# Self-attention of a decoder layer: the values of two steps in one round, one pair of scores ahead of it

## The chip, the core and the metric

The kernel runs on one core of a Trainium2 chip. The metric is the device time of one execution in microseconds (us). The engines of the core are TensorE (PE, with its weight loads shown apart as PEld), VectorE (DVE), ScalarE (ACT), GpSimd (POOL) and SyncE (SP, which here issues transfers).

## The reference, cut to what matters

One decoder layer with layer norms after each part: self-attention with rotary embedding and a linear bias by distance, cross-attention, and a mixture of experts. The change touches the self-attention alone: 4 sequences of 1024 tokens, 16 heads of 16 columns.

```python
B, N, C = x.shape                                    # 4, 1024, 256
q = q * cos + _rotate_half(q) * sin
k = k * cos + _rotate_half(k) * sin
attn = jnp.einsum('bhqd,bhkd->bhqk', q, k) * SCALE
diff = pos[None, :] - pos[:, None]
diff = jnp.where(diff > 0, 0.0, diff)
alibi = diff[None, :, :] * slopes[:, None, None] * MAX_BIAS
attn = attn + alibi[None]
w = jax.nn.softmax(attn, axis=-1)
out = jnp.einsum('bhqk,bhkd->bhqd', w, v)
```

## The kernel before, in words

The stages follow one another: projections, self-attention (`stage_attention`), its output projection, cross-attention, router, experts, combination. Self-attention works on 16 groups, each of four heads of one sequence (`NG`, `HG`), in one window per group. A window has 16 steps (`STEPS`): two halves of 512 queries, and in each half 8 blocks of 128 keys.

In a step, four score tiles (128 keys by 512 queries, one per head, tiles 0 to 3) are computed, exponentiated and multiplied with the values:

- `score_pair` (L741 the product, L755 the bias) writes two tiles. Two heads lie in the two halves of PE's rows, so a pair runs side by side. Steps 0 to 3 and 12 to 15 cross the diagonal and add 6 or 12 small bias products to each tile, 12 or 24 a pair; the other eight steps add none. The tiles go round three banks (`s_ps`, `BANKS`), and `score_main` waits on `exp_done` for the tile three before.
- ACT takes the exponential of each tile (L630) into a set of four buffers, `w_exp`; there are three sets (`SETS`), and the first exponential of a step waits on `pv_done` for the values that last read its set.
- `values` (L782) multiplies the four exponentials of a step with the values into one bank, `a_ps`, summed over a half of the window. The first column beyond the head's 16 is one, so it gathers the softmax's sums.

Softmax subtracts a row's maximum, which has to be known before. So each window also makes the maxima of the next group: 32 units (`max_pair`, L712 the product, L720 the bias), each writing two banks of a ring of two slots, which DVE reduces (`maxima`, L646). Through the same ring pass the transposed tops (`transpose_top`, L770; `copy_top`, L663), sent by `move_top` (L523) into a row of the query stack, and the transposed accumulators (`transpose_acc`, L790; `normalise`, L669 and L673), which ACT has first copied out of `a_ps` (`copy_acc`, L619). The order in which these take the ring's places is written out in `ring_order`, and PE and DVE follow it.

PE's order is written by hand in `window`. Before, in step st: tiles 0 and 1, then the values of step st − 2, then a transpose if one is due, then tiles 2 and 3, then two units of maxima.

Of the kernel before, what the change touches and what calls it, by code (L numbers as in the profile page):

```python
# [408 lines left out]
STEPS = 2 * KT  # L409
TILES = 4 * STEPS  # L410
UNITS = 2 * STEPS
SETS = 3
BANKS = 3


# [8 lines left out]
TOP0_AT = 19  # L424


def ring_order(first, with_max):


    order = []  # L430
    for st in range(STEPS):
        if st == 1:
            order.append(("top", 1))
        if st == 2 and not first:
            order.append(("acc", 1))
        if st == 9 and with_max:
            order.append(("top", 0))
        if st == 10:
            order.append(("acc", 0))
        order += [("max", 2 * st + i) for i in range(2) if with_max]  # L440
    return order


# [18 lines left out]
PLACES = ring_places()  # L462


def stage_attention(nc, io, keep):
# [10 lines left out]
    with Scope(nc, "att") as s:  # L476
# [3 lines left out]
        vg = [s.sb(f"v_group{i}", [P, KT, HG * VW + 32 - VW + 1], F32) for i in range(3)]  # L480
        w_exp = [[s.sb(f"w_exp{i}{h}", [P, CH], F32) for h in range(HG)] for i in range(SETS)]
        ident, past, slope_eye = keep["ident"], keep["past_bf"], keep["slope_eye"]
# [82 lines left out]
        def _(pool):  # L565
# [23 lines left out]
            def window(g, with_max, has_last):  # L589
# [5 lines left out]
                if with_max:  # L595
                    if has_last:

                        pool.wait_ge(pv_done, STEPS * (g.n - 1) + SETS)
                    take_v(g.plus(1))
# [4 lines left out]
        @block.scalar  # L604
        def _(act):
            act.sem_inc(exp_done, BANKS)
            act.sem_inc(acc_done, 1)

            for i in (1, 2):
                for side in range(2):  # L610
                    rows = slice(64 * side + ROW_BIAS, 64 * side + ROW_LOW)
                    for j in range(2):
                        ins = nc.scalar.activation(qs[i][rows, j, :], keep["q_rows"][rows, :], ACT.Copy)
                ins.then_inc(act_prep, 1)

            def copy_acc(g, c):

                act.wait_ge(pv_done, STEPS * g.n + KT * (c + 1) + SETS)
                nc.scalar.activation(acc_sb[c][:, :], a_ps[:, :], ACT.Copy).then_inc(acc_done, 1)  # L619

            def window(g, with_max, has_last):
                for st in range(STEPS):
                    c, kt = divmod(st, KT)
                    for h in range(HG):
                        act.wait_ge(score_done, TILES * g.n + 4 * st + h + 1)
                        if h == 0:

                            act.wait_ge(pv_done, STEPS * g.n + st + 1)
                        v = TILES * g.n + 4 * st + h
                        nc.scalar.activation(w_exp[(STEPS * g.n + st) % SETS][h][:, :], s_ps[v % BANKS][:, :], ACT.Exp).then_inc(exp_done, 1)  # L630
                        if st == 1 and h == 1 and has_last:
                            copy_acc(g.plus(-1), 1)
                        if st == 9 and h == 1:
                            copy_acc(g, 0)

            windows(window)
            copy_acc(Group.of(NG - 1), 1)

        @block.vector
        def _(dve):  # L640
            dve.sem_inc(ring_free, RING_SLOTS)
            def maxima(u, place):
                dve.wait_ge(ring_full, place.at + 1)
                half, j, q, kk = max_unit(u)
                out = row_max[half][:, :, :].rearrange("p (h q) k -> p h q k", q=4)[:, 2 * j:2 * j + 2, q, kk]
                nc.vector.tensor_reduce(out, ring[place.slot][:, :, :], AX.X, ALU.max).then_inc(ring_free, 1)  # L646

            def top_parts(g, half, place):


                dve.wait_ge(ring_free, place.at + 1 + RING_SLOTS)
                nc.vector.tensor_reduce(top[:, :], row_max[half][:, :, :], AX.X, ALU.max).then_inc(top_step, 1)
                dve.wait_ge(top_step, 4 * g.n + 2 * half + 1)
                nc.vector.tensor_scalar(neg_top[:, 0, :], top[:, :], -1.0, None, ALU.mult).then_inc(top_step, 1)
                dve.wait_ge(top_step, 4 * g.n + 2 * half + 2)
                nc.vector.scalar_tensor_tensor(neg_top[:, 1, :], top[:, :], -1.0, neg_top[:, 0, :].bitcast(F32),
                                               ALU.mult, ALU.subtract).then_inc(top_ready, 1)
# [26 lines left out]

            def window(g, with_max, has_last):
                for st in range(STEPS):
                    if st == 1:
                        copy_top(g, 1, PLACES[g.n, "top", 1])
                    if st == 2 and has_last:
                        normalise(g.plus(-1), 1, PLACES[g.n, "acc", 1])  # L690
                    if st == 9 and with_max:
                        copy_top(g.plus(1), 0, PLACES[g.n, "top", 0])
                    if st == 10:
                        normalise(g, 0, PLACES[g.n, "acc", 0])
                    for i in range(2):
                        if with_max:
                            maxima(2 * st + i, PLACES[g.n, "max", 2 * st + i])
                    if with_max and st % 8 == 7:
                        top_parts(g.plus(1), st // 8, PLACES[g.n, "max", 2 * st + 1])

            windows(window)
            last = Group.of(NG - 1)
# [3 lines left out]
        def _(pe):  # L706
            pe.sem_inc(pv_done, SETS)

# [92 lines left out]
            def window(g, with_max, has_last):  # L801
                if with_max:
                    n = g.plus(1)
                    pe.wait_ge(eye_ready, g.n + 2)
                    pe.wait_ge(stack_in[n.buf], 16 * STACK_DMAS * (n.lap + 1))
                for st in range(STEPS):
                    c, kt = divmod(st, KT)
                    if kt == 0:
                        pe.wait_ge(top_in[c], 32 * g.n + 32)
                    score_pair(g, st, 0)  # L810
                    if st > 1:
                        values(g, st - 2)
                    elif has_last:
                        values(g.plus(-1), STEPS + st - 2)
                    if st == 1:
                        transpose_top(g, 1, PLACES[g.n, "top", 1])
                    if st == 2 and has_last:
                        transpose_acc(g.plus(-1), 1, PLACES[g.n, "acc", 1])
                    if st == 9 and with_max:
                        transpose_top(n, 0, PLACES[g.n, "top", 0])  # L820
                    if st == 10:
                        transpose_acc(g, 0, PLACES[g.n, "acc", 0])
                    score_pair(g, st, 2)
                    if with_max:
                        for i in range(2):
                            max_pair(n, 2 * st + i, PLACES[g.n, "max", 2 * st + i])

            windows(window)
            last = Group.of(NG - 1)
# [1656 lines left out]
```

## Time and profile before

| | us |
|---|---|
| median of 3 runs | 2145.97 |
| lowest, highest | 2145.86, 2155.84 |
| the profiled execution, its time | 2138.17 |
| the profiled execution, its span | 2136.4 |

The span is the time from the first to the last instruction of the profiled execution; some 1.8 us of its time lie around it. On the page, PE is busy for 1712.4 us of the span, DVE for 1380.1, ACT for 981.0. Busy time of PE is made of modelled ends of pipelined matmuls, so the starts of its instructions, one after another, tell more than their lengths. A row of the timeline merges like instructions that follow each other: its first number is the start of the first, its second the time to the end of the last.

### The profile page before, as it was taken

The numbers are of one execution on the slowest core, as the hardware profiler recorded it, in microseconds if no ns is written. First come the engines' busy times: TensorE is split into PE (matmuls) and PEld (weight loads), VectorE is DVE, ScalarE is ACT, GpSimd is POOL, SyncE is SP. The second block draws the span as 40 slices with busy tenths as digits, with TensorE's granted clock in tenths as the row PEclk, the third lists the DMA queues.
The fourth block names the chain that finished last, engine by engine and source line by source line (L and its number), as shares of the span: only waits on it lengthen the run. The fifth ranks groups of instructions, "written<-read, shape, count | busy, mean of one in ns | idle before, by whom it ended". The sixth has DMA issues, their size and how long they took to land. (4 is left out here: it accounts for less than half of the span.)

```text
span 2136.4 us, 39383 instructions
## 1 busy us (share of the span) xinstructions
PE 1712.4 (80%) x15124; PEld 1170.3 (55%) x15124; DVE 1380.1 (65%) x2248; ACT 981.0 (46%) x1582; POOL 418.0 (20%) x320
## 2 busy tenths in 40 slices
PE   5747999999999999984656888848874999999900
PEld 5633444444444444433545767726653888888900
DVE  5548888888888888823756787732234566556356
ACT  2312777777777777771212555523332333333100
POOL 4323000000000000001103433301442221111075
PEclk9965999999999999996877999969986999999955
DMA  6687455544445555004533112032222222222055
GB/s 195 148 172 218 66 74 70 72 63 60 59 60 74 72 74 68 16 7 115 180 123 103 57 63 74 24 105 68 87 68 96 82 82 81 81 86 86 25 161 158
DMA packets 135604, 190.89 MB, mean 89 GB/s; under 512 B 32336, under 2 KB 99296, under 8 KB 134436
## 3 DMA queue, kind: packets, MB, share of 16 engines
q1 hardware_dynamic: 128164, 167.02, 34.2%
q0 software_dynamic: 7296, 21.86, 3.2%
q8 instruction: 102, 1.67, 0.4%
q14 instruction: 42, 0.34, 0.1%
HBM read 122.93 MB, written 69.21 MB: 90 GB/s over the span
## 5 line engine op out<-in xcount | busy, mean ns | idle before, releaser
L646 DVE TENSOR_REDUCE att_row_max<-att_ring 128x2 f32<-128x1024 f32 x512 | 602.2, 1220 | 119.3 <-PE att_ring L720 59.6
L630 ACT ACTIVATE att_w_exp<-att_s_ps 128x512 f32<-128x512 f32 x1024 | 547.7, 596 | 232.7 <-PE att_s_ps L755 156.9
L782 PE MATMUL att_a_ps<-att_w_exp,att_v_group 128*32 128x512 f32 x2048 | 273.6, 606 | 0.2 <-ACT att_w_exp L630 0.2
L741 PE MATMUL att_s_ps<-att_q_stack,att_k_stack 62*128 62x512 f32 x640 | 181.4, 480 | 0.0
L741 PEld LDWEIGHTS att_s_ps<-att_q_stack,att_k_stack 62*128 62x128 f32 x640 | 84.3, 184 | 123.9 <-ACT att_w_exp L630 112.7
L2144 ACT ACTIVATE ex_hid<-ex_h_ps,ex_b 128x512 f32<-128x512 f32 x128 | 88.0, 688 | 114.4 <-PE ex_h_ps L2236 72.8
L712 PE MATMUL att_ring<-att_k_stack,att_q_stack 60*128 60x512 f32 x640 | 131.3, 450 | 6.2 <-DVE att_att L673 3.2
L568 POOL COPY att_eyes<-keep_slope_eye 128x384 bf16<-128x384 bf16 x16 | 8.1, 506 | 654.8 <-PE att_s_ps L755 632.4
L755 PE MATMUL att_s_ps<-att_eyes,keep_past_bf 64*128 64x64 bf16 x3840 | 133.0, 193 | 0.0
L741 PE MATMUL att_s_ps<-keep_q_stack,keep_k_stack 62*128 62x512 f32 x384 | 114.1, 487 | 9.9 <-ACT att_w_exp L630 6.3
L712 PE MATMUL att_ring<-keep_k_stack,keep_q_stack 60*128 60x512 f32 x384 | 89.8, 503 | 35.2 <-POOL att_eyes L568 22.0
L1368 POOL TENSOR_TENSOR cr_e<-cr_e,cr_rec 128x1232 f32<-128x1232 f32 x32 | 72.0, 2249 | 221.5 <-DVE cr_rec L1513 221.5
L755 PEld LDWEIGHTS att_s_ps<-att_eyes,keep_past_bf 64*128 64x128 bf16 x3840 | 93.3, 95 | 29.8 <-issue 15.6
L1606 PE MATMUL cr_s_ps<-cr_k_blk,cr_q 128*128 128x308 f32 (+1 forms) x384 | 84.6, 337 | 31.0 <-DVE cr_e L1501 25.6
L2176 DVE CAST ex_h_hi<-ex_hid 128x512 fp32r<-128x512 f32 x128 | 93.6, 732 | 21.4 <-ACT ex_hid L2144 21.1
L2178 DVE TENSOR_TENSOR ex_h_lo<-ex_hid,ex_h_hi 128x512 fp32r<-128x512 f32 x128 | 103.3, 807 | 4.4
L1396 ACT ACTIVATE cr_w_t<-cr_t_ps 77x1024 f32<-77x1024 f32 x64 | 61.9, 1014 | 93.7 <-PE cr_t_ps L1631 93.6
L741 PEld LDWEIGHTS att_s_ps<-keep_q_stack,keep_k_stack 62*128 62x128 f32 x384 | 51.5, 187 | 89.9 <-ACT att_w_exp L630 80.3
L2187 DVE TENSOR_TENSOR ex_y<-ex_y_ps,ex_b 128x256 f32<-128x256 f32 x64 | 26.7, 424 | 111.0 <-PE ex_y_ps L2247 111.0
L1808 POOL DMA_INDIRECT rows_scr<-ro_x_send,ro_put_u x64 | 64.9, 1014 | 152.5 <-DVE ro_put_u L1922 135.5
L2134 ACT ACTIVATE ex_x_hi<-ex_t_ps 128x1024 fp32r<-128x1024 f32 x16 | 16.4, 1026 | 159.5 <-PE ex_t_ps L2224 159.5
L1606 PEld LDWEIGHTS cr_s_ps<-cr_k_blk,cr_q 128*128 128x128 f32 x384 | 66.6, 210 | 41.1 <-issue 22.3
(268 smaller groups left out, 3875.4 us busy)
## 6 DMA issues: line engine op xcount, KB each, us to landing
first_w_raw<-ew SPq DMA_DIRECT2D x16, 1024.0 KB, 7.9
att_k_stack<-qk_scr SPq DMA_DIRECT2D x120, 128.0 KB
keep_k_stack<-qk_scr SPq DMA_DIRECT2D x72, 128.0 KB
qk_scr<-qkv_t_hi SPq DMA_DIRECT2D x64, 128.0 KB, 2.3
qk_scr<-qkv_t_lo SPq DMA_DIRECT2D x64, 128.0 KB, 2.3
rows_scr<-att_zeros POOLq DMA_DIRECT2D x8, 1024.0 KB, 22.0
cr_q<-q_scr SPq DMA_DIRECT2D x16, 512.0 KB, 5.2
ex_rows<-rows_scr SPq DMA_DIRECT2D x16, 512.0 KB, 5.9
```

The costliest lines, as they stand in the source:

```text
L630: nc.scalar.activation(w_exp[(STEPS * g.n + st) % SETS][h][:, :], s_ps[v % BANKS][:, :], ACT.Exp).then_inc(exp_done, 1)
L646: nc.vector.tensor_reduce(out, ring[place.slot][:, :, :], AX.X, ALU.max).then_inc(ring_free, 1)
L712: return nc.tensor.matmul(ring[place.slot][:, i, :], qs[g.buf][rows, j, tok:tok + P], ks[g.buf][rows, half, j, kk * CH:(kk + 1) * CH], sta ...
L741: ins = nc.tensor.matmul(s_ps[v % BANKS][:, :], ks[g.buf][rows, c, j, kt * P:(kt + 1) * P], qs[g.buf][rows, j, c * CH:(c + 1) * CH], start ...
L755: ins = nc.tensor.matmul(s_ps[bank][:, at:at + 64], past[side, far, half, :], eyes[g.buf][side, part, h // 2, :], start=False, stop=n == last)
L782: ins = nc.tensor.matmul(a_ps[32 * h:32 * h + 32, :], vg[g.buf][:, kt, h * VW:h * VW + 32], w_exp[(STEPS * g.n + st) % SETS][h][:, :], sta ...
L1368: pool.tensor_tensor(e[m % 4][:, :, :], e[m % 4][:, :, :], rec[m % 2][:, :].unsqueeze(2).to_broadcast([P, H, L]), ALU.mult).then_inc(w_don ...
L1606: nc.tensor.matmul(s_ps[k][:, half, 0:GL], q[c][a][:, k, tok], k_blk[:, b, bass.ds(i, 1), k, cols].rearrange("p o n -> p (o n)"), start=(j ...
L1808: pool.indirect_dma_start(io["rows_scr"], bass.IndirectOffsetOnAxis(put_u[c][:, 2 * t + k:2 * t + k + 1], 0), x_send[c][:, t, :], None, bo ...
L2144: nc.scalar.activation(hid[m % 2][:, :], h_ps[m % 2][:, :], ACT.Relu, bias=b1[:, bass.ds(e, 1), m:m + 1].rearrange("p a b -> p (a b)") if ...
L2176: nc.vector.tensor_copy(h_hi[c][:, m, :], hid[m % 2][:, :]).then_inc(h_hi_done, 1)
L2178: nc.vector.tensor_tensor(h_lo[c][:, m, :], hid[m % 2][:, :], h_hi[c][:, m, :].bitcast(F32), ALU.subtract).then_inc(h_lo_done, 1)
```

## The change

The values of two steps are computed together, once in two steps, behind tiles 0 and 1 of an even step. Three units of maxima follow the even step's tiles (two) and the odd step's (one), and the fourth is held back: it comes in the next even step, between tiles 0 and 1 and the values (`maxima_ahead`, `maxima_behind`). Transposes move to even steps (tops from 1 and 9 to 2 and 10, accumulators from 2 and 10 to 4 and 12), the copies of the accumulator on ACT from behind tile 1 of steps 1 and 9 to behind tile 2 of steps 0 and 8. `SETS` goes from 3 to 4.

```diff
--- before.py
+++ after.py
@@ -409,7 +409,7 @@
 STEPS = 2 * KT
 TILES = 4 * STEPS
 UNITS = 2 * STEPS
-SETS = 3
+SETS = 4
 BANKS = 3
 
 
@@ -424,20 +424,31 @@
 TOP0_AT = 19
 
 
+def maxima_ahead(st):
+
+    return [2 * st - 1] if st % 2 == 0 and st else []
+
+
+def maxima_behind(st):
+
+    return [2 * st, 2 * st + 1] if st % 2 == 0 or st == STEPS - 1 else [2 * st]
+
+
 def ring_order(first, with_max):
 
 
     order = []
     for st in range(STEPS):
-        if st == 1:
+        order += [("max", u) for u in maxima_ahead(st) if with_max]
+        if st == 2:
             order.append(("top", 1))
-        if st == 2 and not first:
+        if st == 4 and not first:
             order.append(("acc", 1))
-        if st == 9 and with_max:
+        if st == 10 and with_max:
             order.append(("top", 0))
-        if st == 10:
+        if st == 12:
             order.append(("acc", 0))
-        order += [("max", 2 * st + i) for i in range(2) if with_max]
+        order += [("max", u) for u in maxima_behind(st) if with_max]
     return order
 
 
@@ -628,9 +639,9 @@
                             act.wait_ge(pv_done, STEPS * g.n + st + 1)
                         v = TILES * g.n + 4 * st + h
                         nc.scalar.activation(w_exp[(STEPS * g.n + st) % SETS][h][:, :], s_ps[v % BANKS][:, :], ACT.Exp).then_inc(exp_done, 1)
-                        if st == 1 and h == 1 and has_last:
+                        if st == 0 and h == 2 and has_last:
                             copy_acc(g.plus(-1), 1)
-                        if st == 9 and h == 1:
+                        if st == 8 and h == 2:
                             copy_acc(g, 0)
 
             windows(window)
@@ -684,19 +695,24 @@
 
             def window(g, with_max, has_last):
                 for st in range(STEPS):
-                    if st == 1:
+                    if with_max:
+                        for u in maxima_ahead(st):
+                            maxima(u, PLACES[g.n, "max", u])
+                            if u == UNITS // 2 - 1:
+                                top_parts(g.plus(1), 0, PLACES[g.n, "max", u])
+                    if st == 2:
                         copy_top(g, 1, PLACES[g.n, "top", 1])
-                    if st == 2 and has_last:
+                    if st == 4 and has_last:
                         normalise(g.plus(-1), 1, PLACES[g.n, "acc", 1])
-                    if st == 9 and with_max:
+                    if st == 10 and with_max:
                         copy_top(g.plus(1), 0, PLACES[g.n, "top", 0])
-                    if st == 10:
+                    if st == 12:
                         normalise(g, 0, PLACES[g.n, "acc", 0])
-                    for i in range(2):
-                        if with_max:
-                            maxima(2 * st + i, PLACES[g.n, "max", 2 * st + i])
-                    if with_max and st % 8 == 7:
-                        top_parts(g.plus(1), st // 8, PLACES[g.n, "max", 2 * st + 1])
+                    if with_max:
+                        for u in maxima_behind(st):
+                            maxima(u, PLACES[g.n, "max", u])
+                            if u == UNITS - 1:
+                                top_parts(g.plus(1), 1, PLACES[g.n, "max", u])
 
             windows(window)
             last = Group.of(NG - 1)
@@ -808,22 +824,25 @@
                     if kt == 0:
                         pe.wait_ge(top_in[c], 32 * g.n + 32)
                     score_pair(g, st, 0)
-                    if st > 1:
-                        values(g, st - 2)
-                    elif has_last:
-                        values(g.plus(-1), STEPS + st - 2)
-                    if st == 1:
+                    if with_max:
+                        for u in maxima_ahead(st):
+                            max_pair(n, u, PLACES[g.n, "max", u])
+                    if st % 2 == 0 and (st or has_last):
+                        old, at = (g, st) if st else (g.plus(-1), STEPS)
+                        values(old, at - 2)
+                        values(old, at - 1)
+                    if st == 2:
                         transpose_top(g, 1, PLACES[g.n, "top", 1])
-                    if st == 2 and has_last:
+                    if st == 4 and has_last:
                         transpose_acc(g.plus(-1), 1, PLACES[g.n, "acc", 1])
-                    if st == 9 and with_max:
+                    if st == 10 and with_max:
                         transpose_top(n, 0, PLACES[g.n, "top", 0])
-                    if st == 10:
+                    if st == 12:
                         transpose_acc(g, 0, PLACES[g.n, "acc", 0])
                     score_pair(g, st, 2)
                     if with_max:
-                        for i in range(2):
-                            max_pair(n, 2 * st + i, PLACES[g.n, "max", 2 * st + i])
+                        for u in maxima_behind(st):
+                            max_pair(n, u, PLACES[g.n, "max", u])
 
             windows(window)
             last = Group.of(NG - 1)
```

PE in steps of a group without bias products, before: from the values of one step to the values of the next (L741 scores, L712 and L720 maxima, L782 values):

```order
L782 MATMUL att_a_ps<-att_w_exp,att_v_group 32x512 x4
L741 MATMUL att_s_ps<-att_q_stack,att_k_stack 128x512 x2
L712 MATMUL att_ring<-att_k_stack,att_q_stack 128x512 x2
L720 MATMUL att_ring<-att_eyes,keep_past_bf 128x64 x4
L712 MATMUL att_ring<-att_k_stack,att_q_stack 128x512 x2
L741 MATMUL att_s_ps<-att_q_stack,att_k_stack 128x512 x2
L782 MATMUL att_a_ps<-att_w_exp,att_v_group 32x512 x4
```

The same place on PE in the changed program, from one round's values to the next round's (L757 scores, L728 and L736 maxima, L798 values):

```order
L798 MATMUL att_a_ps<-att_w_exp,att_v_group 32x512 x8
L757 MATMUL att_s_ps<-att_q_stack,att_k_stack 128x512 x2
L728 MATMUL att_ring<-att_k_stack,att_q_stack 128x512 x2
L736 MATMUL att_ring<-att_eyes,keep_past_bf 128x64 x4
L728 MATMUL att_ring<-att_k_stack,att_q_stack 128x512 x2
L757 MATMUL att_s_ps<-att_q_stack,att_k_stack 128x512 x4
L728 MATMUL att_ring<-att_k_stack,att_q_stack 128x512 x2
L736 MATMUL att_ring<-att_eyes,keep_past_bf 128x64 x8
L757 MATMUL att_s_ps<-att_q_stack,att_k_stack 128x512 x2
L728 MATMUL att_ring<-att_k_stack,att_q_stack 128x512 x2
L798 MATMUL att_a_ps<-att_w_exp,att_v_group 32x512 x8
```

The values stand there eight matmuls at a time, where before four came after every four score tiles; between two such places there are now eight score tiles and four units of maxima, the last of them right ahead of the values.

ACT at the start of self-attention, before: exponentials (L630) and the first copy of the accumulator (L619):

```order
L630 ACTIVATE att_w_exp<-att_s_ps 128x512 x38
L619 ACTIVATE att_acc_sb<-att_a_ps 128x512
L630 ACTIVATE att_w_exp<-att_s_ps 128x512 x32
```

ACT in the changed program at the same place (L641 exponentials, L630 copy):

```order
L641 ACTIVATE att_w_exp<-att_s_ps 128x512 x35
L630 ACTIVATE att_acc_sb<-att_a_ps 128x512
L641 ACTIVATE att_w_exp<-att_s_ps 128x512 x32
```

The first copy comes three exponentials earlier, behind tile 2 of step 8; between two copies there are 32 exponentials in both.

## Rows read from the trace of the kernel before

**Rows 1.** The page: the span, and the clock of TensorE in 40 slices, tenths.
```profile
span 2136.4 us, 39383 instructions
...
PEclk9965999999999999996877999969986999999955
```

**Rows 2.** Windows: stretch, length, busy PE, PEld, DVE, ACT, POOL, clock, transfers (share, GB/s).
```profile
538.12:585.78 47.66, 47.03 (x590) 22.29 (x594) 40.34 (x45) 35.41 (x67) 1.09 (x2) 1.00 0.45 67
...
919.46:967.20 47.74, 41.22 (x443) 15.25 (x443) 3.50 (x10) 34.93 (x66) 0.00 (x0) 1.00 0.02 8
```

**Rows 3.** Waits in a full window, then in the last one: sum, times, longest, us.
```profile
PEld att_s_ps L741 <- ACT att_w_exp L630: 11.3, 18, 0.8
...
PEld att_ring L712 <- DVE att_row_max L646: 1.0, 2, 0.6
...
PEld att_s_ps L741 <- ACT att_w_exp L630: 22.9, 28, 1.0
```

**Rows 4.** Timeline of PE in a step without bias: start, length, instruction.
```profile
553.55 1.06 PE L782 MATMUL att_a_ps<-att_w_exp,att_v_group 128*32 128x512 f32 x8
554.55 0.50 PE L741 MATMUL att_s_ps<-att_q_stack,att_k_stack 62*128 62x512 f32 x2
554.88 0.40 PE L712 MATMUL att_ring<-att_k_stack,att_q_stack 60*128 60x512 f32 x2
555.12 0.23 PE L720 MATMUL att_ring<-att_eyes,keep_past_bf 64*128 64x64 bf16 x4
...
555.73 0.50 PE L741 MATMUL att_s_ps<-att_q_stack,att_k_stack 62*128 62x512 f32 x1
556.16 1.06 PE L782 MATMUL att_a_ps<-att_w_exp,att_v_group 128*32 128x512 f32 x8
```

**Rows 5.** Timeline of ACT in the same step, and the durations of L630.
```profile
555.08 2.06 ACT L630 ACTIVATE att_w_exp<-att_s_ps 128x512 f32<-128x512 f32 x4 [0.49 <-PE att_s_ps L741]
...
L630 ACT ACTIVATE att_w_exp<-att_s_ps x65: 592/597/618, 538.1 to 585.8; 128x512 f32<-128x512 f32 x65
```

**Rows 6.** Timelines of PE and ACT in a step with bias, last window.
```profile
919.37 1.07 PE L782 MATMUL att_a_ps<-att_w_exp,att_v_group 128*32 128x512 f32 x8
920.37 0.49 PE L741 MATMUL att_s_ps<-keep_q_stack,keep_k_stack 62*128 62x512 f32 x2
...
921.74 0.49 PE L741 MATMUL att_s_ps<-keep_q_stack,keep_k_stack 62*128 62x512 f32 x1 [0.38 <-ACT att_w_exp L630]
...
922.35 1.07 PE L782 MATMUL att_a_ps<-att_w_exp,att_v_group 128*32 128x512 f32 x8
...
921.09 1.08 ACT L630 ACTIVATE att_w_exp<-att_s_ps 128x512 f32<-128x512 f32 x2 [0.55 <-PE att_s_ps L755]
922.44 1.08 ACT L630 ACTIVATE att_w_exp<-att_s_ps 128x512 f32<-128x512 f32 x2 [0.26 <-PE att_s_ps L755]
```

**Rows 7.** Timeline of PE in the router: values-shaped matmuls on end.
```profile
1457.39 1.92 PE L1985 MATMUL ro_l_ps<-ro_hid,ro_rw 128*32 128x512 f32 x16 [0.78 <-ACT ro_hid L1830]
```

**Rows 8.** Timeline of ACT around a copy of the accumulator.
```profile
564.50 0.59 ACT L630 ACTIVATE att_w_exp<-att_s_ps 128x512 f32<-128x512 f32 x1
565.10 0.60 ACT L619 ACTIVATE att_acc_sb<-att_a_ps 128x512 f32<-128x512 f32 x1
565.72 1.08 ACT L630 ACTIVATE att_w_exp<-att_s_ps 128x512 f32<-128x512 f32 x2
```

**Rows 9.** Timelines of DVE and SyncE: tops from copy to transfer.
```profile
518.21 0.27 DVE L663 CAST att_neg_top_t<-att_ring 32x128 fp32r<-32x128 f32 x1
...
524.88 1.24 SPq L523 DMA_DIRECT2D att_q_stack<-top_scr  x2
```

**Rows 10.** Timeline of DVE: one maximum, then two on end.
```profile
555.40 1.23 DVE L646 TENSOR_REDUCE att_row_max<-att_ring 128x2 f32<-128x1024 f32 x1 [0.24 <-PE att_ring L720]
...
521.98 2.35 DVE L646 TENSOR_REDUCE att_row_max<-att_ring 128x2 f32<-128x1024 f32 x2
```

**Rows 11.** A stretch of cross-attention, columns as in rows 2.
```profile
1180.00:1230.00 50.00, 45.41 (x350) 41.07 (x343) 39.93 (x69) 25.55 (x26) 20.92 (x11) 0.97 0.21 72
```

## The prediction

> **What bounds the kernel now.** I read the page first: of the span of 2136.4 us, the slices between about 200 and 970 us are self-attention, with the clock of TensorE (PE) at 9 or more tenths [rows 1]. Cutting that stretch into the 16 windows of the program shows its rhythm. One in the middle has PE busy for 47.0 of 47.7 us, VectorE (DVE) for 40.3 and ScalarE (ACT) for 35.4; so it looks bound by PE. The second row speaks against that. The last window has no maxima to make: DVE falls to 3.5 us and PE to 41.2 us, and the window still takes 47.74 us [rows 2]. So neither PE's amount of work nor DVE sets the time, but something that both kinds of window share.
>
> The waits say what. PE waits for the exponentials (L630) 18 times in a full window, for 11.3 us, and 28 times for 22.9 us in the last one; its weight loads wait for DVE 1.0 us [rows 3]. It is a loop through PE, ACT and the three banks of scores. Call the score tiles of a step 0 to 3. A tile may be written only when the exponential of the tile three before it is done. In a step without bias products [rows 4, 5] the values begin at 553.55; the pair 2, 3 follows at 554.55 (1.00 later); its first exponential starts at 555.08 (0.53 later) and takes 0.60; tile 1 of the next step, which needs that bank, starts at 555.73 (0.05 after it), and the next values at 556.16 (0.43 later). The sum is 1.00 + 0.53 + 0.60 + 0.05 + 0.43 = 2.61 us, which is the whole step. The maxima lie in the wait. In a step with 12 bias products per pair (last window) the same loop reads 1.00, then 0.72 to the exponential, 0.65 to tile 1 at 921.74, where PE visibly waits 0.38, and 0.61 to the values: 2.98 us [rows 6]. Per window, 8 steps have such bias products (0 to 3 and 12 to 15) and 8 have none.
>
> **The change part by part.** No instruction is added or taken away. What changes is how often values stand between scores.
>
> *Two steps' values together.* The switch is cheaper: 128 times in place of 256 does PE go from scores to values and back. One step of values is two passes of four matmuls, 1.06 us in all [rows 4]. The router has matmuls of the same shape, and there four passes on end take 1.92 us [rows 7]: the two further passes cost 0.86, where a step that stands alone takes 1.00. But the loop gets longer. Take a round without bias, with t = 0 at the pair 2, 3 of the even step, right behind the double values. Until the next double values, PE must write eight tiles: 2, 3 of the even step, 0 to 3 of the odd one, 0 and 1 of the next even one. Tile 1 at the end needs the bank of tile 2 of the odd step, so five exponentials must have run: the first starts at 0.53, and four in a row take 2.06 us, so they follow each other by (2.06 − 0.60)/3 = 0.49 [rows 5]. The fifth starts at 0.53 + 4 × 0.49 = 2.49 and ends at 3.09; tile 1 starts at 3.14. Behind it stand the held-back maxima, a pair that costs 0.24 (554.88 to 555.12) [rows 4], and 0.43 to the values as before: 3.81. The double values take 1.00 + 0.86: **5.67 us a round, where two steps now take 5.22: +0.45**. The two exponentials that run under the double values fill 1.1 of its 1.9 us; ACT idles for the rest and lacks it afterwards.
>
> In a round with bias, t = 0 at the same place: first exponential at 0.72; tile 1 of the odd step waits for it until 0.72 + 0.60 + 0.05 = 1.37. A tile waited for in this way has its pair's first exponential 0.70 later (921.74 to 922.44), at 2.07 [rows 6]; tile 3 waits for that one until 2.72, the exponential of tile 2 starts at 3.42, and the next tile 1 waits for it until 4.07. From there 0.61 to the values, and about 0.3 for the maxima pair between (0.24 to 0.33, the two distances in [rows 4]): 4.98. With 1.86 of values: **6.84, against 2 × 2.98 = 5.96: +0.88**. One loop through ACT per step has become three per round. Steps with 24 bias products lengthen both sides alike.
>
> Four rounds of each kind give 4 × (0.45 + 0.88) = 5.3 us a window.
>
> *Copies of the accumulator.* They move from behind tile 1 of the odd steps 1 and 9 to behind tile 2 of steps 0 and 8, that is, into the run of exponentials that sets the time. One holds ACT from 565.10 to 565.72, 0.6 us [rows 8]. Before, it also stood in a row of exponentials, so part of that was paid already. Between 0 and 1.2 us a window, I take 0.4.
>
> *The held-back maxima* are in the sum above (0.24 or 0.3). In the last window there are none, so it grows by 4 × (0.45 − 0.24) + 4 × (0.88 − 0.3) + 0.4 = 3.6 us.
>
> *Fourth set of exponentials.* The first exponential of a step waits for values four steps back and not three. That wait is not among those listed [rows 3], so it is worth nothing. *Transposes* of tops and accumulators move one or two steps later and still stand behind values on PE: same cost. The transfer of the tops that follows, from the copy at 518.21 to the end of the last issue at 526.12 [rows 9], takes 8 us and was due at step 16 from step 9, some 20 us; with six steps left (some 16 us) it is still early, and so is SyncE's queue behind it. GpSimd's copies wait for whole windows and have a window's slack.
>
> Sum: 15 × (5.3 + 0.4) + 3.6 = **+89 us**, all in self-attention. Against the profiled execution, 2138.2 + 89 = 2227; the median of the runs stands 7.8 us above that execution, so I forecast **2235 us**, 4.1% slower. Ends of the sum: copies free and the held-back maxima at half their price (the other half under tile 1), 15 × 4.2 + 3.2 = 66; copies in full, 15 × 6.5 + 4.4 = 102.
>
> **The rivals.**
>
> *The cheaper switch decides (faster).* Where PE never waits for an exponential, each double round saves the cold entry of one values step: 1.00 − 0.86 = 0.14, the way into it (0.43 against 0.33 from pair to pair) and out of it (a first pair of 0.33 against 0.24) [rows 4]: about 0.33 × 128 = 42 us, 2104 us. The Trainium skill, "TensorEngine Tiling (Array Packing)", section "Key Properties", says that changing the tiling mode drains TensorE; by that rule alone the time would be these 2104 us. The trace agrees that the switch costs, with the distances just read. It decides from the point where the exponentials keep up with eight tiles on end. Against it stands the last window, where 6 us less work on PE gave nothing [rows 2].
>
> *The maxima's ring becomes the bound (slower still).* Two slots hold the maxima, and the held-back pair needs the slot of the one two before it. In a round without bias the first maxima start about 0.33 after t = 0, DVE begins 0.52 later (554.88 to 555.40) and needs 2.35 for two [rows 4, 10]: the slot is free at 3.25, and the held-back pair's turn comes behind tile 1 at 3.14, whose own 0.24 covers the rest. 0.2 us more per round would be 24 us: 2259.
>
> *The clock falls (slower still).* PE would idle about as in the last window, where the clock stayed at 1.00 [rows 2]; in cross-attention, with PE busy for 45.4 of 50 us, it was 0.97 [rows 11]. Three per cent on some 850 us is 25 us at most: 2260. The skill's "TensorE: Matmul & The Clock Gate", section on psum-queue depth-cycling, names short idle times between groups of matmuls as a cause of such falls.
>
> *Nothing happens.* The loop is absorbed in the waits that PE has now, 11.3 us a window [rows 3]: 2146. That would need ACT to run further ahead than three banks let it.
>
> **How the numbers follow.** Forecast 0.74, ring 0.10, clock 0.08: slower by over 0.5%, which is about what a measurement of this kernel can tell from no change, 0.92. Nothing 0.04, faster 0.04. The range takes in the lower end of the sum on the lower base (2138 + 66 = 2204) and the two slower rivals with some room (2259 and 2260): 2204 to 2265. The upper end of the sum on the higher base, 2146 + 102 = 2248, lies inside.
>
> **What would show it.** After the change, windows of self-attention of some 53 us, PE busy for less of them, ACT at 35 us as before; a round without bias of 5.7 us, two runs of values touching, and in the gap two exponentials; waits of score tiles for L630's successor at 20 us or more a window; DVE idle longer. Wrong is the forecast if windows get shorter than 47.7 us, if the long waits are DVE's for PE or PE's for DVE, or if the clock leaves 1.00. Right in the total but wrong in its parts would be rounds with bias that grow no more than those without.

## The result, and the profile after

The changed kernel takes 2255.3 us (median of 4 runs, 2250.89 to 2260.16) against 2145.91 us: the ratio is 1.051, with a 95% interval of 1.0455 to 1.0565. The forecast was 2235 us, in a range of 2204 to 2265.

The page of the changed kernel, the lines that answer to [rows 1]:

```profile
span 2257.4 us, 39383 instructions
...
PEclk9966999999999999999686899977996999999955
```

Self-attention's slices still read 9 tenths. Each digit is the mean of a slice of 56 us, and it hides something, as the windows show. They are cut at the first exponential of each group, with the columns of [rows 2]:

```profile
477.05:531.81 54.76, 52.40 (x590) 25.22 (x594) 40.85 (x45) 34.45 (x66) 1.09 (x2) 0.97 0.41 58
...
584.98:638.12 53.14, 50.81 (x590) 24.77 (x594) 40.73 (x45) 34.45 (x66) 1.09 (x2) 1.00 0.41 60
1019.88:1075.00 55.12, 48.58 (x439) 18.65 (x443) 3.52 (x10) 34.36 (x66) 0.00 (x0) 0.91 0.02 7
```

There are two lengths of full windows. Three take 53.15 us at a clock of 1.00, 5.5 us more than before. Eleven take 54.8 us or so, and their clock is 0.97. The first takes 56.0 us (from 49.6); it starts at a low clock in both kernels, and shows the same fall as the eleven. The last window, up to the end of its values (the row above stops 0.7 us earlier), takes 55.8 us (from 47.7) at 0.91.

A round without bias in the changed kernel, the timelines of PE and then of ACT (steps 6 and 7 of the group that begins at 584.98), which answer to [rows 4, 5]:

```profile
605.43 1.92 PE L798 MATMUL att_a_ps<-att_w_exp,att_v_group 128*32 128x512 f32 x16
607.28 0.51 PE L757 MATMUL att_s_ps<-att_q_stack,att_k_stack 62*128 62x512 f32 x2
...
610.43 0.50 PE L757 MATMUL att_s_ps<-att_q_stack,att_k_stack 62*128 62x512 f32 x1
610.56 0.60 PE L728 MATMUL att_ring<-att_k_stack,att_q_stack 60*128 60x512 f32 x2
611.09 1.92 PE L798 MATMUL att_a_ps<-att_w_exp,att_v_group 128*32 128x512 f32 x16
...
604.10 2.08 ACT L641 ACTIVATE att_w_exp<-att_s_ps 128x512 f32<-128x512 f32 x4
607.82 4.03 ACT L641 ACTIVATE att_w_exp<-att_s_ps 128x512 f32<-128x512 f32 x8 [1.65 <-PE att_s_ps L757]
```

From values to values it is 611.09 − 605.43 = 5.66 us; the working gave 5.67. The values of two steps take 1.85 us to the next pair (1.86). The bracket on ACT's second row is the price: ahead of eight exponentials on end, 4.03 us, ACT has had nothing to do for 1.65 us. From the start of the last tile ahead of the values to the first exponential behind them it is 0.66 + 1.85 + 0.54 = 3.05 us (610.43 to 611.09, 605.43 to 607.28, 607.28 to 607.82), and the three banks hold three exponentials for that time, at 0.49 us each. Before, ACT waited 0.49 us in each step.

The twelve windows with a fall differ from the three at one place, around the values of step 10. The timeline of PE, first in such a window, then in one of the three:

```profile
509.88 3.04 PE L798 MATMUL att_a_ps<-att_w_exp,att_v_group 128*32 128x512 f32 x16
512.85 0.29 PE L786 MATMUL att_ring<-keep_ident,att_neg_top 128*32 128x128 f32 x1
...
564.17 1.92 PE L798 MATMUL att_a_ps<-att_w_exp,att_v_group 128*32 128x512 f32 x16
566.02 0.28 PE L786 MATMUL att_ring<-keep_ident,att_neg_top 128*32 128x128 f32 x1
```

The same 16 matmuls take 1.1 us longer. The stretch shows why (three pieces of it):

```profile
502.00:505.40 3.40, 3.40 (x35) 1.29 (x32) 3.30 (x6) 1.92 (x4) 0.00 (x0) 1.00 1.04 128
505.40:508.80 3.40, 2.92 (x19) 1.38 (x16) 2.79 (x4) 3.23 (x7) 0.00 (x0) 0.99 1.04 124
508.80:512.20 3.40, 3.40 (x19) 1.23 (x23) 2.10 (x2) 1.28 (x3) 0.00 (x0) 0.50 0.58 75
```

PE's clock is at 0.50 (1.2 GHz, not 2.4) from 508.8 to 512.2. Ahead of it lies step 9, where PE was busy for 2.92 of 3.40 us; it stood for 0.48 us in front of a score tile:

```profile
507.20 0.98 PE L757 MATMUL att_s_ps<-att_q_stack,att_k_stack 62*128 62x512 f32 x2 [0.48 <-ACT att_w_exp L641]
```

A window with this fall is 1.62 us longer, and there are 12 of them in this execution.

So the sum is: 15 full windows by 5.5 us, 82.5; 12 falls by 1.62, 19.4; the last window 8.1. That is 110 us. From the end of attention's values (967.2 before, 1075.7 after) the trace gives 108.5, and the medians 109.4.

### The profile page after: what moved, and what is told of

It is laid out like the page before. It is cut to its first block and busy times, and to the rows that moved or that the text cites. A ratio compares the mean times of both kernels' runs of the same rounds, so it can differ in the third digit from the quotient of the medians.

```text
span 2257.4 us, 39383 instructions
## 1 busy us (share of the span) xinstructions
PE 1795.6 (80%) x15124; PEld 1213.1 (54%) x15124; DVE 1386.3 (61%) x2248; ACT 965.1 (43%) x1582; POOL 416.0 (18%) x320
## 5 line engine op out<-in xcount | busy, mean ns | idle before, releaser
L641 ACT ACTIVATE att_w_exp<-att_s_ps 128x512 f32<-128x512 f32 x1024 | 539.0, 610 | 356.1 <-PE att_s_ps L771 216.2
L798 PE MATMUL att_a_ps<-att_w_exp,att_v_group 128*32 128x512 f32 x2048 | 267.9, 644 | 0.2 <-ACT att_w_exp L641 0.2
L757 PE MATMUL att_s_ps<-att_q_stack,att_k_stack 62*128 62x512 f32 x640 | 246.2, 487 | 22.9 <-ACT att_w_exp L641 21.1
L757 PEld LDWEIGHTS att_s_ps<-att_q_stack,att_k_stack 62*128 62x128 f32 x640 | 102.5, 184 | 136.6 <-ACT att_w_exp L641 101.8
L757 PE MATMUL att_s_ps<-keep_q_stack,keep_k_stack 62*128 62x512 f32 x384 | 151.8, 496 | 20.2 <-ACT att_w_exp L641 16.8
L728 PE MATMUL att_ring<-att_k_stack,att_q_stack 60*128 60x512 f32 x640 | 164.3, 455 | 0.6
L771 PE MATMUL att_s_ps<-att_eyes,keep_past_bf 64*128 64x64 bf16 x3840 | 150.7, 193 | 0.0
L728 PE MATMUL att_ring<-keep_k_stack,keep_q_stack 60*128 60x512 f32 x384 | 106.9, 508 | 33.2 <-POOL att_eyes L579 22.9
L771 PEld LDWEIGHTS att_s_ps<-att_eyes,keep_past_bf 64*128 64x128 bf16 x3840 | 102.9, 95 | 33.0 <-issue 25.1
L798 PEld LDWEIGHTS att_a_ps<-att_w_exp,att_v_group 128*32 128x32 f32 x2048 | 56.1, 115 | 113.2 <-ACT att_w_exp L641 56.3
L757 PEld LDWEIGHTS att_s_ps<-keep_q_stack,keep_k_stack 62*128 62x128 f32 x384 | 62.5, 188 | 92.9 <-ACT att_w_exp L641 68.7
```

What stands on the lines that cost most here:

```text
L728: return nc.tensor.matmul(ring[place.slot][:, i, :], qs[g.buf][rows, j, tok:tok + P], ks[g.buf][rows, half, j, kk * CH:(kk + 1) * CH], sta ...
L757: ins = nc.tensor.matmul(s_ps[v % BANKS][:, :], ks[g.buf][rows, c, j, kt * P:(kt + 1) * P], qs[g.buf][rows, j, c * CH:(c + 1) * CH], start ...
L771: ins = nc.tensor.matmul(s_ps[bank][:, at:at + 64], past[side, far, half, :], eyes[g.buf][side, part, h // 2, :], start=False, stop=n == last)
L798: ins = nc.tensor.matmul(a_ps[32 * h:32 * h + 32, :], vg[g.buf][:, kt, h * VW:h * VW + 32], w_exp[(STEPS * g.n + st) % SETS][h][:, :], sta ...
```

## The experiments

Times of windows are from the traces. They are the better measure here, since the rest of the program, behind attention, which no version changes, takes from 1169 to 1188 us in these executions.

### The copies, and what makes the clock fall

`copies_late`: the copies move behind tile 2 of the odd step, the tile whose bank the last tile ahead of the values waits for.

```diff
-                        if st == 0 and h == 2 and has_last:
+                        if st == 1 and h == 2 and has_last:
                             copy_acc(g.plus(-1), 1)
-                        if st == 8 and h == 2:
+                        if st == 9 and h == 2:
                             copy_acc(g, 0)
```

> The changed kernel with ACT's two copies of the accumulator behind tile 2 of steps 1 and 9 in place of steps 0 and 8. Theory (the time is a run of exponentials through three banks, plus a fall of PE's clock at step 10 in 12 of 15 windows): the copy leaves the run that the last tile ahead of the values waits for, so a window at full clock takes 52.0 us and not 53.2; PE's long wait in step 9 shrinks by the 0.6 us of the copy, and the falls at step 10 become fewer or none. Total 17 us (clock as it is) to 40 us (no falls) below the changed kernel. Rival (copies are free, the ring of maxima binds): windows stay at 53.2 and 54.8 us, total the same within 5 us.

Measured: 2238.84 us (2230.44 to 2244.06), 1.0401 of the kernel before (1.0353 to 1.0448). Full windows take 52.55 us, and none has a fall:

```profile
530.00:582.60 52.60, 50.60 (x586) 24.68 (x586) 40.68 (x45) 34.59 (x68) 1.09 (x2) 1.00 0.44 61
991.00:1054.10 63.10, 57.26 (x449) 20.37 (x443) 3.66 (x10) 34.46 (x66) 0.00 (x0) 0.78 0.02 6
```

At full clock the copies cost 0.6 us a window (53.15 to 52.55), half of what was expected of them, and the falls went with them. The last window, though, grew to 63.0 us at a clock of 0.78. The total is 16.5 us below that of the changed kernel by the medians, 23 us by the ratios to the kernel before; 17 to 40 were expected. The rival (copies free) is out.

`filled`: more work for PE, in the place where it waits (the edit, cut):

```diff
+FILL = {16: 1, 17: 2, 18: 1}
...
                 pe.wait_ge(ring_free, place.at + 1)
+                for again in range(FILL.get(u, 0)):
+                    for i in range(2):
+                        max_main(g, u, i, place, stop=True)
                 for i in range(2):
                     ins = max_main(g, u, i, place)
```

> The changed kernel with four more pairs of PE products per window, in the waits of steps 8 and 9: the product of maxima units 16 and 18 is made twice, that of unit 17 three times, into the same place, so the result stays. Theory (the clock falls because PE waits too much there): more work on PE, and the kernel gets faster: no fall at step 10, all full windows at 53.2 to 53.5 us, attention 12 x 1.6 = 19 us shorter, total 2236 us. Rival (the falls come from elsewhere, or PE's work binds): windows of 54.8 us remain, or each window grows by up to 4 x 0.24 = 1 us, total 2255 to 2270 us.

Measured: 2247.79 us (2244.84 to 2259.07). Every full window but the first is at 53.22 to 53.26 us, with a clock of 1.00:

```profile
531.00:584.20 53.20, 51.15 (x595) 25.29 (x595) 40.71 (x45) 34.52 (x67) 1.09 (x2) 1.00 0.43 59
1004.00:1071.80 67.80, 61.93 (x447) 21.77 (x443) 3.62 (x10) 34.38 (x66) 0.00 (x0) 0.70 0.02 5
```

More work on PE took the fall out of all windows that had one, and the extra products cost 0.1 us a window. So the waits that were filled have a part in the falls. They are not the whole of it: `no_hold` below keeps the wait of 0.48 us in step 9, PE is busy for less of a window (49.3 of 52.1 us, against 50.8 of 53.1), and no full window has a fall:

```profile
545.49 0.99 PE L757 MATMUL att_s_ps<-keep_q_stack,keep_k_stack 62*128 62x512 f32 x2 [0.48 <-ACT att_w_exp L641]
```

The total fell by 7.5 us where 19 were expected; the intervals of the two ratios overlap, so the total alone does not show a gain. The last window, which this edit does not touch, took 67.7 us at a clock of 0.70. Over all versions with three banks and double values the last window took 55.7 to 67.7 us, the longer the more of it ran at 0.50.

### The parts of the regrouping

`no_hold`: both units of maxima of an odd step follow it; none waits for the next round (the edit, cut).

```diff
-    return [2 * st - 1] if st % 2 == 0 and st else []
+    return []
...
-    return [2 * st, 2 * st + 1] if st % 2 == 0 or st == STEPS - 1 else [2 * st]
+    return [2 * st, 2 * st + 1]
```

> The changed kernel without the held-back maxima: both units of an odd step follow it at once. Theory (the held-back pair stands on the path, 0.24 us in a round without bias and 0.3 with): a window at full clock takes 52.1 us, 1.1 less than 53.2, total some 16 us below the changed kernel, a few more or less by the clock. Rival (holding it back spares a wait for DVE's reductions): windows longer than 53.2 us, and waits of PE for DVE above those of the changed kernel.

Measured: 2231.5 us (2230.69 to 2235.86), 1.0385 (1.0341 to 1.0429); full windows 52.05 us, with no fall. The pair did stand on the path, at 1.1 us a window. Not in every round, though: the round of steps 6 and 7 grew, from 5.65 to 5.78 us, while that of 14 and 15 fell from 7.13 to 6.73. In the traces attention ends 34.0 us earlier than in the changed kernel (1075.7 to 1041.7): 16 were expected, and most of the rest are the falls, which were not expected to go. The medians are 23.8 us apart.

`late_no_hold`: the edits of `copies_late` and `no_hold` together.

> The changed kernel with both the copies behind tile 2 of steps 1 and 9 and no held-back maxima. Theory (the two lie on the path one after the other, though not in all rounds apart): a full window takes 51.4 us, no fall of the clock in it, and the values of two steps on end alone cost 3.7 us a window against the kernel before. Rival (each only cured the fall of the clock): 52.0 us or more, as with one of them.

Measured: 2221.42 us (2215.99 to 2226.56), 1.0346 (1.0301 to 1.0391); full windows 51.91 us. That is nearer to the rival: 0.15 us below `no_hold` alone. The two do not add, 0.6 and 1.1 giving 1.25. What is left against the kernel before, 4.26 us a window, is what the values of two steps on end cost, with the moved transposes, when copies and held-back maxima are out of the way; 3.7 was expected.

`sets_three`: `SETS = 3` in the changed kernel.

> The changed kernel with three sets of exponentials in place of four. Theory (the wait for a free set never ends last): windows at full clock 53.2 us, with a fall of the clock 54.8 us, total the same within 5 us. Rival (the fourth set pays for part of the regrouping): windows longer than 55 us.

Measured: 2258.21 us (2251.57 to 2264.31), full windows 53.13 to 53.16 or 54.73 to 54.82 us, and the first 56.04. The fourth set does nothing for the time. Eleven windows have the fall here, twelve in the changed kernel, eight in `half_reduce`: their number moves between versions whose windows are otherwise alike.

### Does the ring of maxima bind?

`half_reduce`: DVE reduces every second column.

```diff
-                nc.vector.tensor_reduce(out, ring[place.slot][:, :, :], AX.X, ALU.max).then_inc(ring_free, 1)
+                nc.vector.tensor_reduce(out, ring[place.slot][:, :, ::2], AX.X, ALU.max).then_inc(ring_free, 1)
```

> The changed kernel with DVE reducing only every second column of each bank of maxima; half of the keys is left out of the maxima. Theory (DVE is not on the path): a reduction takes about 0.7 us in place of 1.2, DVE's busy time per window falls from 40.7 to about 24 us, and the windows stay at 53.2 and 54.8 us; total the same within 5 us. Rival (the ring of maxima binds): windows shorter by 0.2 us a round or more, total at least 24 us below.

Measured: 2260.0 us (2256.09 to 2265.56). DVE has 24.3 us to do in a window where it had 40.7, and windows take the same, 53.17 us or 54.8 with a fall. One without, and then DVE's reductions in the whole execution:

```profile
636.27:689.45 53.18, 50.81 (x590) 24.62 (x594) 24.30 (x45) 34.45 (x67) 1.09 (x2) 1.00 0.44 60
...
L657 DVE TENSOR_REDUCE att_row_max<-att_ring 128x2 f32<-128x512 f32 x512 | 340.5, 689 | 373.6 <-PE att_ring L736 212.4 <-PE att_ring L728 160.4
```

A reduction takes 689 ns, and DVE stands idle ahead of them for 373.6 us in all, for PE. This rival of the prediction is out.

### Is it the three banks?

`five_single` and `five_double` give five banks to the scores, in the kernel before and in the changed one. The maxima of every second head are left out of both, main products and bias products, and zeros stand for them. Both carry this edit (cut):

```diff
-BANKS = 3
+BANKS = 5
...
-        ring = [s.pb(f"ring{i}", (P, 2, 512)) for i in range(RING_SLOTS)]
+        ring = [s.pb(f"ring{i}", (P, 1, 512)) for i in range(RING_SLOTS)]
...
-                for i in range(2):
+                for i in range(1):
                     ins = max_main(g, u, i, place)
```

> The kernel before with five banks of scores in place of three. The banks come from the ring of maxima, whose slots have one bank: the maxima of every second head are left out (a zero stands for them), and DVE reduces half as much. Theory (three banks of scores bind, in both orders): a full window falls from 47.7 to about 42.7 us, the last one to about 36 us, and PE's waits for exponentials nearly vanish. Rival (PE's work binds): a full window falls only by what the smaller ring takes from PE, under 1 us.

> The changed kernel with the same five banks of scores and the same half of the maxima left out. Theory (values of two steps on end cost time because three banks hold too little for ACT meanwhile): a full window falls from 53.2 (54.8 with a fall of the clock) to about 44.5 us, so that the change costs about 1.8 us a window with five banks, where it costs 5.5 to 7.1 with three; the total is 30 to 45 us above that of the kernel before with five banks. Rival (the double round costs for a reason that has nothing to do with the banks): it stays 5 us or more a window above, 80 us or more in all. Rival (the cheaper switch decides once PE no longer waits): it is faster than the kernel before with five banks.

Measured: 2068.49 us (2062.14 to 2078.88), 0.9658 of the kernel before (0.9613 to 0.9703), and 2073.99 us (2067.59 to 2083.42), 0.9682 (0.9638 to 0.9726). A full and the last window of the first, then of the second:

```profile
491.00:534.14 43.14, 42.98 (x517) 20.26 (x515) 23.62 (x44) 34.95 (x67) 1.09 (x2) 1.00 0.48 69
854.00:890.60 36.60, 35.83 (x443) 13.85 (x435) 2.53 (x9) 33.17 (x66) 0.00 (x0) 1.00 0.03 10
```

```profile
491.00:534.20 43.20, 42.98 (x515) 21.69 (x514) 24.02 (x44) 33.60 (x66) 1.09 (x2) 1.00 0.52 73
851.70:894.20 42.50, 39.98 (x443) 15.56 (x435) 2.37 (x9) 33.34 (x67) 0.00 (x0) 1.00 0.03 9
```

In a full window the same regrouping costs 0.06 us with five banks, where it costs 5.5 with three. That is less than the 1.8 us expected, and the totals are 5.5 us apart where 30 to 45 were expected. The maxima left out do not explain it. `half_reduce` has shown that DVE's smaller share is not what did it for the changed kernel. PE's smaller share is no candidate either: the two products of a unit ran side by side. From the first product of two units to the tile behind them it is 0.67 us in the kernel before (554.88 to 555.55) and 0.67 us in `five_single` (528.95 to 529.62). The expectation that PE's waits for exponentials nearly vanish was not met: the weight loads of `five_single` wait 10.1 us for ACT in a full window (11.3 before).

The 0.06 us is a balance, not the absence of a cost. Its rounds are between 0.85 us shorter and 0.80 us longer than in `five_single`. And in the last window, at a clock of 1.00 in both, the regrouping still costs 5.8 us (36.64 to 42.47). A round without bias there, PE and then ACT of `five_double`, then ACT of `five_single`:

```profile
867.12 2.11 PE L802 MATMUL att_a_ps<-att_w_exp,att_v_group 128*32 128x512 f32 x16
869.16 0.96 PE L761 MATMUL att_s_ps<-keep_q_stack,keep_k_stack 62*128 62x512 f32 x5
870.34 1.48 PE L761 MATMUL att_s_ps<-keep_q_stack,keep_k_stack 62*128 62x512 f32 x3 [0.22 <-ACT att_w_exp L642]
...
869.69 4.03 ACT L642 ACTIVATE att_w_exp<-att_s_ps 128x512 f32<-128x512 f32 x8 [0.60 <-PE att_s_ps L761]
...
861.43 11.05 ACT L631 ACTIVATE att_w_exp<-att_s_ps 128x512 f32<-128x512 f32 x22
```

In `five_single` ACT makes exponentials there without a break and sets the time. In `five_double` it stands for 0.60 us in such a round. The account is the same as with three banks: from the start of the last tile ahead of the values (871.32) to the first exponential behind them (874.32) it is 3.0 us, and five banks hold 5 × 0.49 = 2.45 us of work for ACT. In the full windows PE's own work, some 4.6 us in two steps without bias in `five_single`, hides that loop; that is read from the traces, and no run separates it. So the banks set the price of the regrouping in a full window, and five of them take nearly all of it away there, but not where ACT sets the time. The rival by which the cheaper switch would win, once PE no longer waits, is not borne out: the changed kernel is not the faster one here. It is not put to the full test either, since PE's weight loads still wait for ACT in both.

`one_bank_slots` and `one_bank_double` try to have the five banks with all the maxima: slots of one bank, each unit made and reduced as two (the edit, cut).

```diff
-            def max_pair(g, u, place):
+            def max_pair(g, u, places):
...
+                for i in range(2):
+                    pe.wait_ge(ring_free, places[i].at + 1)
+                    ins = max_main(g, u, i, places[i])
```

> The kernel before with five banks of scores and nothing left out: the ring's two slots have one bank each, and every unit of maxima becomes two, one per head, each reduced by itself. Theory (the three banks of scores set the time): faster than both kernels. DVE now has 64 reductions of about 0.60 us a window, 39 us, and some 3 us of other work, so a full window lies between the 43.1 us of five banks with half the maxima and the 47.7 us of the kernel before; I expect 44 to 46 us, the last window 36.6 us, total 35 to 65 us below the kernel before. Rival (DVE and the smaller slots bind instead): full windows of 47 us or more, and only the last window shorter, total within 15 us of the kernel before.

> The changed kernel with the same five banks of scores and slots of one bank, nothing left out. Theory (the change's cost comes from the three banks): the distance to the kernel before with these slots is under 2 us a window where it is 5.5 to 7.1 with three banks; DVE gets its units less evenly, so some of it stays. Rival (values of two steps on end cost time whatever the banks): 5 us or more a window.

Measured: 2558.39 us (2549.1 to 2581.79), 1.1874 (1.1794 to 1.1953), and 2625.51 us (2620.97 to 2630.99), 1.2193 (1.212 to 1.2265). A clear miss. Full windows of the first take 69 to 82 us (those over 71 us at a clock of 0.77 to 0.91), with PE, DVE and ACT all idle for a part of it (a stretch as long as one window, then the waits from 500 to 545):

```profile
500.00:570.00 70.00, 56.35 (x598) 24.82 (x601) 44.88 (x78) 36.36 (x67) 1.09 (x2) 1.00 0.34 46
```

```profile
PEld att_ring L717 <- DVE att_row_max L652: 14.7, 21, 1.2
...
PE att_ring L717 <- DVE att_row_max L652: 8.0, 11, 0.8
```

Two slots of one bank hold one unit and no longer two. The weight loads of the maxima stand for DVE 21 times in these 45 us, for 14.7 us, with scores and values queued behind. Only the last window, which has no maxima, got its gain (38.3 us from 47.7). The banks that the scores lack cannot simply come from the ring. In their full windows these two say nothing more on the change, since another wait governs them. In the last window they agree with the five banks above: 38.3 us before the regrouping and 46.0 after, at clocks of 0.96 and 0.92. No version that computes all of it beat the kernel before.

## Why the prediction was right

**The bound.** Right, and the five banks show it: with them the full window of the kernel before falls from 47.65 to 43.14 us, and the last from 47.75 to 36.64. That PE's share of busy time (98.7% of a window) was no bound was read from the last window, [rows 2].

**A round without bias, +0.45.** Right: 5.66 us measured from values to values, 5.67 worked out, 5.22 before. That is the round the working was made for; the four of this kind differ widely, as below.

**A round with bias, +0.88.** Right in kind and near in size: steps 14 and 15 take 4.42 + 2.71 = 7.13 us by the first exponentials, where they took 3.17 + 2.99 = 6.16: +0.97. Over a window at full clock the four rounds with bias grow by 0.50, 0.49, 1.62 and 0.98, 3.6 us where 3.5 were forecast, and the four without by 1.16, 0.44, 0.25 and 0.06, 1.9 us where 1.8 and the copies' 0.4 were. The sums of the two kinds hold; single rounds do not, since copies, transposes and maxima fall into some of them, and that they even out is luck.

**The sum of a window, 5.7 us.** 5.5 at full clock. Its parts were less exact than the sum. The held-back maxima were priced at 4 × (0.24 + 0.3) = 2.2 us a window and are worth 1.1; the copies at 0.4, and they are worth 0.6; so the values on end cost more (4.26) than the working had for them without the held-back pair (5.3 − 2.2 = 3.1). Two errors of about 1 us a window cancel.

**The clock.** This is the term that was mis-sized: the sum has nothing for it. The prediction had it as a rival, at 25 us at most and a chance of 0.08, in place of the sum; it came on top of it, with 19 us in the full windows and a part of the 4.5 us by which the last window exceeds its 3.6. The evidence taken, a clock of 1.00 in the last window before, was the wrong place: there PE waits 0.4 us at a time, spread over the steps. In step 9 of the changed kernel the copy of the accumulator comes ahead of the exponential that PE stands 0.48 us for, and four tiles in a row then start one by one, 0.49 us apart, behind an exponential each. The sum should have been 89 and some 20. The prediction named a clock that leaves 1.00 as a sign that the forecast is wrong, and by that sign it was wrong in this term: 0.97 in a window with a fall, 0.91 in the last.

That the range held 2255 is in part luck. Its sum alone ends at 2248; the room above came from the two slower rivals, of which the ring did not happen and the clock came on top of the sum, not in its place. The rival's 3% was read from cross-attention. It fits the 1.62 us in 53.15 that a fall costs here, but nothing in the traces ties the two numbers together.

**The signs to look for.** Windows of some 53 us, values that touch, ACT at 35 us, DVE idle for longer: all there. Rounds with bias grew by more than those without, as they had to. Waits of score tiles at 20 us or more a window are not there:

```profile
ACT att_w_exp L641 <- PE att_s_ps L771: 11.2, 15, 2.4
PEld att_s_ps L757 <- ACT att_w_exp L641: 10.2, 26, 0.8
ACT att_w_exp L641 <- PE att_s_ps L757: 7.4, 4, 2.2
```

They are 10.2 us for the weight loads in a full window (11.3 before, [rows 3]), in more pieces (26 in place of 18). The growth shows on the other side, with ACT, which waits 18.6 us for PE, up to 2.4 at a time (12.4 before). A loop that is too long may show in either engine of it.

**Rivals.** The ring of maxima: refuted by `half_reduce`. The cheaper switch: real in size (1.85 us for the values of two steps in place of 2 × 1.00), not decisive in any run here; with five banks full windows come out even. Nothing happens: refuted by the result.

## What to carry to other kernels

Where an engine hands tiles to another through a few banks, set the time for which it is away, from its last tile to the other's first work on the next, against the work that the banks hold for the other. Here 3.05 us stood against 1.47, with five banks 3.0 against 2.45, and the difference, 1.6 and 0.55, is about what ACT lost in a round (1.65 and 0.60). Work gathered into longer runs, however cheap each run becomes, is paid for where that difference is what sets the time; where another engine's work is longer, it hides. Take away work that shares the stretch, as the last window did here, or add a bank, before believing that a busy engine is the bound. And price the clock together with a change that makes an engine wait longer, since it comes on top.

## What the runs showed of the hardware that was not expected

The fall of PE's clock does not follow from PE's idle time at a place alone. In a window without a fall, the stretch that answers to 505.4 to 508.8 is the same, PE busy for 2.92 of 3.40 us, and the clock stays:

```profile
560.16:563.56 3.40, 2.92 (x19) 1.38 (x16) 2.79 (x4) 3.23 (x7) 0.00 (x0) 1.00 1.01 118
563.56:566.96 3.40, 3.40 (x30) 1.39 (x30) 2.30 (x3) 1.48 (x4) 0.00 (x0) 1.00 0.42 60
```

The moment of the fall drifts against the program. Counted from a window's first exponential, it comes at 32.4 us in the second window and a little earlier in each that follows, at 31.7 in the sixth; the next three have none; in the tenth it comes at 32.5, and at 31.7 again in the fifteenth. `filled` shows that the waits it fills have a part in the fall, and `no_hold` that such a wait can stand without one. What spared three windows is not shown. Nor is why the last window of the versions ran between 10 and 40 us at the lower clock (worked out from its mean clock, 0.91 of 55.8 us to 0.70 of 67.7 us, as time at 1.00 or 0.50).
